# Gathers and results on one queue: POOL issues all twenty gathers before the first result

## What is computed

```python
probs = softmax(xf @ gate_w.T + gate_b)            # xf: 2048 tokens x 128, layer-normed
topw, topi = top_k(probs, 2)                       # two experts of 8 for each token
sel_w, sel_idx = top_k(wm.T, cap)                  # each expert takes its cap = 307 best tokens
xg = xf[sel_idx]                                   # 8 x 307 x 128
h = gelu(einsum('ecd,edh->ech', xg, w1) + b1)      # 8 x 307 x 512
out = einsum('ech,ehd->ecd', h, w2) + b2
of = zeros(2048, 128).at[sel_idx].add(out * sel_w) # a token may get up to two results
t = t + of
```

## Time and profile before

| | us |
|---|---|
| median of 3 runs | 160.93 (160.16 to 161.36) |
| the profiled execution | 160.53 |
| its span, first to last instruction | 158.8 |
| POOL busy | 70.8 (45% of the span) |
| PE busy | 122.4 (77%) |
| experts' stage, first `up` to the end of PE | 87.8 to about 144.9 |

### The profile page before, as it was taken

How to read it: one execution, slowest core, us unless ns; L and a number is a source line. 1 busy time by engine, 2 the same in 40 slices (tenths; PEclk the granted TensorE clock), 3 DMA queues, 4 the chain that set the end, 5 groups by cost and what they waited for, 6 DMA issues and landing times.

```text
span 158.8 us, 2492 instructions
## 1 busy us (share of the span) xinstructions
PE 122.4 (77%) x855; PEld 92.8 (58%) x855; DVE 85.4 (54%) x332; ACT 52.0 (33%) x141; POOL 70.8 (45%) x124
## 2 busy tenths in 40 slices
PE   6699999998795876779775899799491999994000
PEld 2377999997661443344673687687460868874000
DVE  2567789776779888878751104163201435334361
ACT  4299777661179700000000324045001340450000
POOL 7985365457340000002077767567772524356100
PEclk9999999999999789999965599999969789999755
DMA  3579999500000000082002221202120000115597
GB/s 116 141 187 401 301 301 399 208 0 4 0 0 2 4 0 0 0 265 55 0 19 56 60 56 47 58 33 58 54 56 33 20 32 17 33 45 165 169 278 222
DMA packets 15596, 15.46 MB, mean 97 GB/s; under 512 B 1816, under 2 KB 12224, under 8 KB 15584
## 3 DMA queue, kind: packets, MB, share of 16 engines
q1 hardware_dynamic: 14240, 12.45, 25.1%
q0 software_dynamic: 1344, 2.86, 6.3%
HBM read 9.67 MB, written 5.64 MB: 96 GB/s over the span
## 4 chain that ended last, share of the span: by engine, by line
PE 43%; issue 22%; ACT 9%; another core or an unknown queue 8%; DMA 7%; POOL 3%; DVE 3%; SPq 3%; POOLq 0%; DVEq 0%
PE bank L1131 14%; PE bank L1115 10%; PE bank L946 4%; ACT rows L569 4%; DMA xb<-parts 3%; PE bank L973 2%; PE bank L986 2%; DMA vecs<-in_L_conv_k_beta_dram 2%; PE bank L976 2%; PE bank L941 2%; DMA parts<-y_tail,tail_rows 1%; PE bank L959 1%; ACT hid L588 1%; PE bank L1109 1%
## 5 line engine op out<-in xcount | busy, mean ns | idle before, releaser
L1131 PE MATMUL bank<-w_sb,hid 128*128 128x128 f32 (+1 forms) x192 | 27.7, 298 | 6.3 <-ACT hid L588 3.4
L1131 PEld LDWEIGHTS bank<-w_sb,hid 128*128 128x128 f32 (+1 forms) x192 | 23.7, 178 | 8.7 <-DVE y_tail L880 3.5
L588 ACT ACTIVATE hid<-bank,b1T 128x307 f32<-128x307 f32 x32 | 15.6, 518 | 38.9 <-PE bank L1115 26.5
L481 POOL DMA_INDIRECT parts<-q_work,kv x16 | 15.7, 980 | 16.7 <-DVE q_work L880 13.3
L923 PE MATMUL bank<-warm_rhs 128*128 128x512 bf16 x76 | 21.3, 412 | 1.4 <-POOL warm_rhs L359 1.4
L1115 PE MATMUL bank<-xgT,w_sb 128*128 128x307 f32 x64 | 21.2, 480 | 0.6 <-ACT xgT L574 0.6
L463 POOL DMA_INDIRECT kv<-table,index x16 | 16.5, 1033 | 10.0 <-DVE index L850 5.4
L880 DVE SCALAR_TENSOR_TENSOR q_work<-bank,kv,wb 128x128 f32<-128x128 f32 x16 | 5.6, 351 | 23.7 <-PE bank L1131 21.3
L1115 PEld LDWEIGHTS bank<-xgT,w_sb 128*128 128x128 f32 x64 | 13.1, 217 | 6.6 <-issue 3.8
L1050 PEld LDWEIGHTS bank<-hits,ones 128*128 128x128 bf16 x160 | 6.1, 102 | 12.7 <-DVE hits L779 10.1
L494 POOL DMA_INDIRECT w_h<-table,first_rows x1 | 1.2, 1189 | 27.4 <-DMA table<-rows 27.4
(11 more groups left out here) (197 smaller groups left out, 238.2 us busy)
## 6 DMA issues: line engine op xcount, KB each, us to landing
w_sb<-in_L_ffn_w_dram SPq DMA_DIRECT2D x1, 2048.0 KB, 10.5
parts<-zeros SPq DMA_DIRECT2D x4, 512.0 KB, 7.7
table<-rows SPq DMA_DIRECT2D x1, 1152.0 KB, 5.9
x_sb<-parts SPq DMA_DIRECT2D x4, 256.0 KB, 3.1
xb<-parts SPq DMA_DIRECT2D x4, 256.0 KB, 4.5
out_dram<-att SPq DMA_DIRECT2D x4, 256.0 KB, 2.5
x_sb<-in_x_dram SPq DMA_DIRECT2D x1, 512.0 KB, 4.6
b_sb<-in_L_ffn_b_dram SPq DMA_DIRECT2D x1, 512.0 KB, 18.3
```

The costliest lines, as they stand in the source:

```text
L481: pool.indirect_dma_start(out=parts, out_offset=bass.IndirectOffsetOnAxis(ap=xg_rows[:, e // 2, at, C + E + e:C + E + e + 1], axis=0), in_ ...
L588: act.activation(hid[:, e % 2, c, :], ps_h[c][:, 0:CAP], ACT.Gelu, bias=b1T[:, e * HC + c:e * HC + c + 1]).then_inc(h_ready, 1)
L1131: ins = pe.matmul(ps_ys[(NC * e + k) % 2][y_at:y_at + n, 0:C], hid[:, e % 2, c, at:at + n], w2_sb[:, e, c, :], start=(c == 0), stop=(c == ...
```

## The change

The tuple with the counts goes. POOL now issues all twenty gathers in the same order as before, and then runs `put(0)` to `put(7)`. What each gather and each result waits for, reads and writes stays as it was, and so do all other engines.

```diff
-    GATHERS_AFTER = (10, 3, 4, 3)
...
             order = []
             for e in range(0, E, 2):
                 order += [(e, c) for c in range(LAST)] + [(e + 1, LAST)] + [(e + 1, c) for c in range(LAST)]
-            assert sum(GATHERS_AFTER) == len(order)
-            done = 0
-            for e in range(-1, E):
-                if e >= 0:
-                    put(e)
-                n = GATHERS_AFTER[e + 1] if e + 1 < len(GATHERS_AFTER) else 0
-                for next_e, c in order[done:done + n]:
-                    gather(next_e, c)
-                done += n
+            for e, c in order:
+                gather(e, c)
+            for e in range(E):
+                put(e)
```

## The result

The changed kernel is slower: 167.55 us (166.89 to 169.57, 4 runs) against 161.15 us (160.16 to 164.31, 4 runs) of the kernel before on the same chip. The ratio is 1.0405, with a 95% interval of 1.0327 to 1.0483. The profiled execution took 166.89 us with a span of 165.1 (before: 160.53 and 158.8).

The account below looks back on a forecast made before the run. PE's expert chain was taken as the bound, delayed by late completions during POOL's unbroken issue. Losses of 10.7 plus 2.9 us for the clock, less 10.6, gave +3.0: span 161.8, time 163.5 us, range 153 to 168.

Parts of the forecast that it names:

- POOL's unbroken issue: POOL issuing indirect DMAs without breaks, taken to make PE's completions reach other engines late, by 5 and 6 us at worst.
- the heavy lag: Likeliest case: PE slowed to rate 0.44 until POOL catches up, +3.0 us net, range 161.5 to 167, chance 0.42.
- the low clock: PE's granted clock at 0.50 (1.2 GHz) behind idling, making one expert's `up` and `down` 2.9 us longer.
- The earlier gathers: Ten gathers come forward, the twentieth ending at 105.7 us; gain 0, since only the first gather was ever waited for.
- The later results: Results go behind the gathers, first at 106.0 instead of 94.49 us; cost 0, covered by 8 us and more of PE's work.
- second episode: Rival: behind the catch-up PE and POOL meet again at nearly full issue, losing 4.1 us more, 168 us; chance 0.09.
- r = 0.44: PE's assumed rate while POOL issues unbroken: one expert's 5.66 us of work done in 12.84 us.
- the large episode: In the kernel before, late PE completions filling 111 to 122.5 us, beside POOL's nearly unbroken issue from 104.04 to 120.34.
- The forecast's own formula: POOL catches up with the results 12.5 / (1 - 0.60 r) us behind 93.5, r being PE's rate.
- the drain of 2.1 us: Time after POOL stops issuing until PE's completions are no longer late; put the lag's end at 112.6 us.
- 10.6: Microseconds PE lost in the kernel before, mainly in the second, fourth and fifth experts, over 5.66 us each; subtracted from new losses.
- The page that spoke against it: Skill page by whose rule POOL's order would leave PE alone and the change would come to 0.

## Why the prediction was right, and where its sum fell short

**The mechanism held.** The forecast named POOL's unbroken issue as what makes PE's completions late, and the heavy lag as the likeliest case. Moving, replacing and breaking up POOL's stretch moved, removed and shrank the lag, while 16-byte rows, memsets and SP's traffic told it from its neighbours. The signs that the forecast gave came: gathers unbroken, the first result at 105.73 (forecast 106.0), DVE and ACT late from the first `down` on, PE waiting over 10 us (all in the second expert, where the forecast had the second and third), the low clock behind it. The size was off: the profiled execution rose by 6.4 us where the sum said 3.0, and 167.55 us lies just inside the stated 153 to 168.

**The pieces costed at nothing were worth nothing.** The earlier gathers gained 0: the only wait of PE for one is again 1.3 us. The later results cost 0: the end is 19.28 us behind the last `up` in both. And no second episode came. POOL had a break of about 2 us or more for every expert from 119 us on (2.68, 3.44, 2.15 us and so on), which the pauses show to be enough.

**The term that was mis-sized: PE's rate.** The sum took r = 0.44 from the large episode. Measured in the same way, from `down` to `down` (92.59 to 112.04, 19.45 us for 5.66), it was 0.29. The forecast had PE do 8.4 us of work in 19.1 us and lose 10.7; from 93.5 to its restart at 112.04, 18.5 us, it did only 5.2 and lost 13.33. The forecast's own formula with 0.29 has POOL catch up at 108.6 (it stopped at 108.01), and with the drain of 2.1 us PE would lose 12.2 us. So the end of the episode came out nearly right (112.04 for 112.6) by two errors against each other: a slower PE makes fewer results, which stops POOL earlier, and behind the stop ACT got its counts only after 3.37 us and not 2.1, with another 0.66 us to PE's start.

A rate is also the wrong picture. In an unbroken stretch a count gets through once in 3 to 9 us (DVE's in this kernel at 94.25, 100.83 and 109.97, in the run with one break at 106.59, 111.53 and 119.24, ACT's in the run with memsets at 124.39, 127.20 and 130.03), and PE does what the counts at hand allow, here to 98.71, and then nothing.

**The other terms.** The low clock cost 5.52 - 3.06 = 2.46 us where 2.9 were forecast. The first expert took 1.33 us more than before, where the forecast had 0. That isn't the order: the run with one break and the one with 16-byte rows have the same order up to 92 us, and took 7.39 and 7.38 for it (87.80 to 95.19, 87.76 to 95.14). The granted clock rose later in this execution: from 90 to 92 us it was 0.50 here, 0.66 in the run with one break and 0.81 before. Why it did is open. The sum with measured terms is 13.33 + 2.46 + 0.08 + 1.33 - 10.6 = 6.6, where the forecast had 3.0.

**The page that spoke against it.** The Trainium skill, page "SBUF — State Buffer", section "SBUF: two separate sides", has PE and ACT wait on no one. This case's trace doesn't contradict it for memory accesses: PE's own matmuls kept their length (24 in 3.06 us at 97.87 in the run with one break) beside POOL's issuing. What came late was their completion, by 13.9 us, and of that the section tells nothing.

**What stays open.** No run names the part of the chip that holds the counts back, nor whether PE's results are written late or only their counts travel late: the ends of matmuls are modelled, and only the starts of the next ones are seen. The runs say what it takes: indirect DMAs from POOL on end, and many small matmuls. The traces also show that it hits PE's counts, and not those that DVE and ACT send to PE. In the kernel before, inside the large episode, DVE took a chunk late and its own count was with PE at once:

```profile
113.98 0.35 DVE L880 SCALAR_TENSOR_TENSOR q_work<-bank,kv,wb 128x128 f32<-128x128 f32 x1 [2.33 <-remote]
```

DVE ends at 114.33, and PE starts at 114.39, with POOL unbroken from 104.04 to 120.34. ACT's count in the run with memsets was as quick. Whether the number of rows of a DMA matters, whether it is matmuls or weight loads that count, and whether it is the same with matmuls of other types, wasn't tried.

## What to carry to other kernels

Where one engine issues indirect DMAs in a long row beside dense matmuls, look for consumers of PE that start late with "remote" as the releaser, and set the issuing engine's timeline beside them. If the two go together, break the row up: pauses of 2 us after every fifth DMA cost POOL 10 us, gave the changed kernel 9, and left it 2.4% faster than the kernel before. Spreading the gathers among the results gave 1.8% without a pause; try that first. And a rate read from an episode that the change will lengthen is a poor term; ask how far the waiting engine can get on what it already has.

## What the runs showed of the hardware

- PE's completion counts reached DVE and ACT up to 13.9 us late while POOL issued one indirect DMA each 1.25 us. The first of them to come behind POOL's stop came 1.4 to 3.0 us after its last issue (1.96 in the changed kernel, 1.99 with one break, 2.48 with 16-byte rows, 3.00 beside SP's traffic, 1.61 with the late start, 1.37 with the `up` in 24 matmuls, 1.82 with pauses of 2 us, 2.13 before); some took up to 3.7.
- DVE's and ACT's counts reached PE at once in the same stretches: 0.06 us from DVE's end to PE's start before (114.33 to 114.39), and 0.06 from ACT's in the run with memsets (127.72 to 127.78).
- It came with 2 GB/s moved as with 58, and with results alone as with gathers. It didn't come with 171 GB/s of SP's DMAs, nor with 10 us of memsets on POOL.
- It needs dense matmuls to begin, as far as one run each can show: 8 in an `up` of 4.43 us passed unharmed 17 us into POOL's row, and 24 in one of 5.41 us didn't.
- In a row that begins beside a dense PE, delays of 0.6 to 1.4 us stand from 5 to 6 us in, after four or five DMAs, and larger ones from 7 to 9 us in. 2 us of pause cleared them and 1 us didn't.
- An indirect DMA costs POOL mostly 0.94 to 1.0 us and 0.30 to the next, with rows of 16 bytes as with rows of 576; the first of a row took up to 1.2, and the second gather 2.0.
